# Convolution, attention and a sorted graph layer on one core: six images first, the gathers spread over four stages

## What is computed

```
def reference(x, ...):                      # x: (8, 56, 56, 64), float32
    # 1. 32 paths of 1x1 conv 64->4, 3x3 conv 4->4, 1x1 conv 4->64, each with batch norm and relu; summed
    x = relu(sum_over_paths(path(x)) + x)
    t = x.reshape(8, 3136, 64)
    # 2. attention, 8 heads, a 7 x 7 window around each pixel
    t = t + attention(layernorm(t))
    # 3. graph attention over 262144 random edges (src, dst < 16384), then a mixture of 4 experts
    z = layernorm(t).reshape(25088, 64)
    h = (z @ W_gat).reshape(M, HEADS, NUM_EXPERTS)
    a_src, a_dst = (h * att_src).sum(-1), (h * att_dst).sum(-1)
    e = leaky_relu(a_src[src] + a_dst[dst])             # every edge, and a loop on every node
    ee = exp(e - segment_max(e, dst)[dst])
    alpha = ee / segment_sum(ee, dst)[dst]
    agg = segment_sum(h[src] * alpha, dst) + b_gat
    w, k = top2(layernorm(agg).mean_over_heads)         # gates of two of four experts
    return t + sum_over_experts(gate[e] * (gelu(z @ W1[e] + b1[e]) @ W2[e] + b2[e]))
```

## Time and profile before

| | |
|---|---|
| median of 3 runs | 6876.4 us (6873.09 to 6878.02) |
| the profiled execution: time, span | 6868.53 us, 6867.0 us |
| busy PE, PEld | 2998.4 us, 2106.3 us |
| busy DVE, ACT, POOL | 3009.2 us, 1471.6 us, 3021.5 us |
| gathers L1483: busy, idle ahead of them | 2008.8 us, 990.0 us |

### The profile page before, as it was taken

One profiled execution on the slowest core, in us unless ns is written; L12 is line 12 of the kernel. 1 busy time (PEld: TensorE's weight loads), 2 busy tenths in 40 slices (PEclk: granted clock), 3 DMA queues, 4 the chain that ended last, 5 costly groups with the idle time before them and its releaser, 6 DMA issues. The chain is left out here.

```text
span 6867.0 us, 61389 instructions
## 1 busy us (share of the span) xinstructions
PE 2998.4 (44%) x16592; PEld 2106.3 (31%) x16592; DVE 3009.2 (44%) x4102; ACT 1471.6 (21%) x5678; POOL 3021.5 (44%) x3316
## 2 busy tenths in 40 slices
PE   2888888879999450000444231313121131314400
PEld 1444454468888340000333120202111120203200
DVE  5888888559999321011999020201111020202229
ACT  0333333468888220000000010100000010101100
POOL 1000000046767237776000767575757667572345
PEclk9788888779999555555555555555555555555555
DMA  6666666556666331000000011111111111111125
GB/s 138 89 92 94 96 95 96 83 90 102 103 101 102 87 91 8 9 7 7 3 4 3 13 46 16 33 24 33 28 32 25 15 46 15 34 24 47 49 70 198
DMA packets 584829, 385.88 MB, mean 56 GB/s; under 512 B 404739, under 2 KB 531507, under 8 KB 581715
## 3 DMA queue, kind: packets, MB, share of 16 engines
q1 hardware_dynamic: 385528, 221.54, 14.5%
q10 hardware_dynamic: 89403, 109.89, 9.2%
q0 software_dynamic: 109728, 52.69, 6.6%
HBM read 235.34 MB, written 147.70 MB: 56 GB/s over the span
## 5 line engine op out<-in xcount | busy, mean ns | idle before, releaser
L1483 POOL DMA_INDIRECT e_row<-scratch_table,e_edge x2048 | 2008.8, 981 | 990.0 <-issue 681.8
L1664 PE MATMUL f_psY<-f_w,f_hid 128*128 128x64 f32 x1568 | 363.1, 425 | 1649.5 <-ACT f_hid L1615 1052.8
L1547 DVE TENSOR_TENSOR f_y<-f_psY,f_b 128x1024 f32<-128x1024 f32 x49 | 59.8, 1220 | 2294.7 <-DMA scratch_vpad<-v 1432.9
L1664 PEld LDWEIGHTS f_psY<-f_w,f_hid 128*128 128x128 f32 x1568 | 342.6, 330 | 1741.9 <-ACT f_hid L1615 1117.1
L1522 DVE TENSOR_TENSOR i_hot<-f_psH,i_digit 128x1024 bf16<-128x1024 f32 x512 | 582.4, 1214 | 639.9 <-DMA scratch_b<-c_b3p 371.6
L1615 ACT ACTIVATE f_hid<-f_psH,f_b 128x512 f32<-128x512 f32 x196 | 131.4, 687 | 2920.5 <-PE f_psH L1659 1352.0
L1647 PE MATMUL f_psH<-i_hot 128*128 128x128 bf16 x2048 | 264.8, 310 | 958.2 <-DVE i_hot L1522 814.5
L947 POOL MEMSET a_wproj<- 128x128 f32 x1 | 0.2, 210 | 1368.4 <-POOLq L144 1368.4
L1060 ACT ACTIVATE prob<-psS,low 128x100 f32<-128x100 f32 x1568 | 514.1, 373 | 62.1 <-DVE low L1093 62.0
L1647 PEld LDWEIGHTS f_psH<-i_hot 128*128 128x128 bf16 x2048 | 197.2, 140 | 1025.7 <-DVE i_hot L1522 879.4
L455 PE MATMUL psH<-h,c_w 128*128 128x448 f32 x1008 | 508.7, 592 | 3.6 <-ACT h L567 1.8
(11 more groups left out here) (280 smaller groups left out, 5385.6 us busy)
## 6 DMA issues: line engine op xcount, KB each, us to landing
stack<-scratch_parts ACTq DMA_DIRECT2D x504, 112.0 KB
e_row<-scratch_table,e_edge POOLq DMA_INDIRECT x2048
scratch_y<-f_y ACTq DMA_DIRECT2D x49, 512.0 KB
g_y<-scratch_y SPq DMA_DIRECT2D x28, 896.0 KB, 4.9
scratch_state<-e_state SPq DMA_DIRECT2D x16, 1536.0 KB, 6.0
val<-scratch_vpad SPq DMA_DIRECT2D x672, 35.0 KB
scratch_parts<-h2p ACTq DMA_DIRECT2D x56, 336.0 KB, 3.8
keys<-scratch_kpad SPq DMA_DIRECT2D x112, 155.0 KB
```

The lines of the kernel that those rows point to most:

```text
L1483: pool.indirect_dma_start(out=row[s][:, f, :], out_offset=None, in_=table_dram, in_offset=bass.IndirectOffsetOnAxis(ap=edge[s][:, 0, f:f + ...
L1664: m = pe.matmul(psY[par][:, j, e * C:(e + 1) * C], hid[e][:, j * 128:(j + 1) * 128], w2[:, e, :], start=True, stop=True)
```

## The change

Images 0 to 5 go through convolution, attention and the table first (`FIRST_IMAGES = 6`). The rows that edges need are then all in the table. Images 6 and 7 go through the same three stages a second time, and POOL gathers meanwhile. The parts:

- A class `Gather` deals with the 2048 gathers in 32 units of 64. A unit has its list of sources (3 lists in a ring), one of 4 row buffers, and a store to DRAM. Four units run beside the second convolution, three beside the second attention, one beside the second table, eight beside the counting, and the last 16 after the scatter. The scans read the rows back from DRAM with SP's queue (`load_rows`).
- Weights of the convolution stay in the on-chip memory, so that the second call prepares nothing.
- In the second attention POOL does nothing but gather: SP loads all 10 rows of values, the residual's rows and stores the result.
- The sort has 11 slots a tile; its 429 steps after the prefix then need 39 tiles where they needed 48.
- The table stage is unrolled, with rings of 4 buffers in place of pairs, and the index steps stand between the steps of its chunks on DVE. In the second call squares and scaling are on DVE.
- Join and output are one stage, `finish_phase`: four blocks of columns, (128,196), (0,48), (48,96), (96,128); the first needs no gathered sums. Sums stay on the chip. Scaling, a sum by halves, and the residual are all on DVE, in chunks of 8.

```diff
-SORT_SLOTS = (5, 6, 7, 8, 9, 10, 11, 12, 13)
+SORT_SLOTS = (4, 5, 6, 7, 8, 9, 10, 11, 12, 13, 14)
...
+FIRST_IMAGES = 6
+UNIT = FC // 2
+UNITS = 2 * NFC
+CONV_UNITS, ATTENTION_UNITS, TABLE_UNITS, COUNT_UNITS = 4, 3, 1, 8
...
+    def gather(self, pool, count):
+
+        for unit in range(self.unit, self.unit + count):
+            if unit == 0:
+                for k in range(self.LISTS):
+                    self.load_list(pool, k)
+            s = unit % self.SLOTS
+            pool.wait_ge(self.list_in[unit % self.LISTS], 16 * (unit // self.LISTS + 1))
+            wait(pool, self.rows_out[s], 16 * (unit // self.SLOTS))
+            for f in range(UNIT):
+                pool.indirect_dma_start(out=self.row[s][:, f, :], out_offset=None, in_=self.table,
+                                        in_offset=bass.IndirectOffsetOnAxis(ap=self.list[unit % self.LISTS][:, f:f + 1].bitcast(I32), axis=0)
+                                        ).then_inc(self.rows_in[s], 16)
+            if unit > 0:
+                self.store(pool, unit - 1)
...
-    conv_phase(nc, io, t1, q, kpad, vpad, ordered)
-    attention_phase(nc, io, t1, q, kpad, vpad, t2)
-    index_phase(nc, io, ordered, digit, edge, first, ends)
-    table_phase(nc, io, t2, z, table, adst)
-    edge_phase(nc, io, z, table, adst, digit, edge, node, first, b, state, y)
-    join_phase(nc, io, state, node, first, ends, sums)
-    output_phase(nc, io, table, adst, sums, y, t2, out)
...
+            held = ConvWeights(nc, ctx)
+            conv_phase(nc, io, held, early, t1, q, kpad, vpad, sorted_dram=ordered)
+            attention_phase(nc, io, early, t1, q, kpad, vpad, t2, lasting=lasting)
...
+                table_phase(nc, io, early, t2, z, table, adst, index=index)
+            rows = Gather(nc, ctx, lasting, table[0:FIRST_IMAGES * H * W], edge, gathered)
+            conv_phase(nc, io, held, late, t1, q, kpad, vpad, rows=rows, units=CONV_UNITS)
+            attention_phase(nc, io, late, t1, q, kpad, vpad, t2, rows=rows, units=ATTENTION_UNITS)
+            table_phase(nc, io, late, t2, z, table, adst, rows=rows, units=TABLE_UNITS)
+            edge_phase(nc, io, rows, z, adst, digit, edge, node, first, b, state, y)
+        finish_phase(nc, io, state, node, first, ends, table, adst, y, t2, out)
```

More of the change, by code:

```diff
@@ L1280, in _ @@
+                for r in range(RING):
+                    sp.wait_ge(stored[r], stores(r + (COUNT - 1 - r) // RING * RING))
+                if index is not None:
+                    index.stored_all(sp)
             @block.vector
@@ L1500, in _ @@
                 pool.dma_start(b_dram.rearrange("(p x) h -> p x h", p=128)[:, 0, :], b_first[:]).then_inc(b_placed, 16)
[L1501 to L1503 removed]
+                rows.gather(pool, UNITS - rows.unit)
             @block.vector
```

1164 lines of the change are left out of this document (674 added, 490 removed).

## The result

The changed kernel takes 6906.91 us (6875.72 to 6911.66, 20 runs) beside 6869.66 us for the kernel before (6860.32 to 6880.72, 20 runs): ratio 1.0051, 95% interval 1.0044 to 1.0059. It is slower by half a per cent. The forecast was 6870, six microseconds less than before; the range held, the sign did not. On some (those numbered 11 and 12 on record), PE, ACT, DVE and SP are slowed while POOL gathers; on others (0, 1 and 2) they are not. I call the first the slowing kind and the others the free kind. Chip 2 was met at two times and chip 11 at two times, and each showed its kind again. Both kernels were first measured on the slowing kind.

What follows compares the result with a forecast made beforehand. Gathers were taken as almost serial, with PE at about a tenth of its rate beside them. The terms -244 - 206 - 140 + 637 + 528 + 145 - 571 - 155 = -6 gave 6870 us, range 6515 to 6980.

Steps and rivals of the forecast that it cites:

- first scores: Start of attention's scores after the early convolution of 42 tiles, 39 of them sorting: at 1172.9 us, a gain of 244.
- second convolution: Convolution of the last images beside 256 gathers: 3 + 347 + 11 + 276 = +637 us.
- second attention: Attention of the last images beside 192 gathers, SP bounding a strip at 8.4 us: 263 + 11 + 254 = +528 us.
- second table: Table stage of the last images beside 64 gathers and a store: 88, 11 and 46, together +145 us.
- edge stage, first gather to last tile: Counting, scatter, 1024 later gathers at 1364 us with stores, then 34 tiles at 15.53: 3313 us, a gain of 571.
- What bounds the kernel: Whole kernel: gathers hide little, PE at 10% of its rate in counting, 14% in tiles; their 2700 us almost serial.
- three terms: Work done beside the moved gathers: 71 us in second convolution, about 34 in second attention, 20 in second table.
- the sort: Early convolution: two more slots lengthen a sorting tile by 1.3 us, from 22.3 to 23.6 (23.1 to 24.5).
- The gather's price in the tiles: Edge stage behind the scatter: 1024 gathers at 1.304 us each and 16 stores at 1.8, together 1364 us.
- The table's chunk: Early table, with four buffers and shifted steps: 5.1 us a chunk (4.85 to 7.8), 117 for the stage, -102.
- Rival one: Slowdown belongs to the edge stage's loops; unrolled convolution and table run free: 6526, chance 0.08; attention too: 6289, chance 0.05.
- Rival two: Gathers in second convolution and attention queue behind other transfers, 1.6 us for 1.35: 7087, with half 6979; chance 0.12.

Runs made afterwards that it cites:

- e3: The kernel before with eleven sort slots a tile in place of nine, nothing else: 5938.3 us beside 5857.5, ratio 1.0132, on the free kind.
- e4: The changed kernel without the split, with nine slots and the kernel before's edge stage, on the free kind: 5612.5 us beside 5857.5 for the kernel before.
- e9: The same program as e4 on the slowing kind: 6624.7 us beside 6874.7 for the kernel before, ratio 0.9633.
- small stages: A program of its own without the layer's work, short unrolled pieces side by side, such as PE beside gathers: 1707.0 us on the free kind, 1871.4 on the slowing.
- e8: The changed kernel with its eight early units of gathers put behind the scatter, on the slowing kind: 6936.1 us beside 6874.7 for the kernel before.
- e16: The changed kernel with a 500-column memset behind every edge gather, small stages behind it, slowing kind: 8464.1 us in all, the layer done at 6357.5.

## Why the prediction was right and wrong

| step | forecast | measured | difference |
|---|---|---|---|
| first scores | 1172.9 | 1208.9 | +36 |
| first attention, first to last scores | 618 | 617 | -1 |
| from there to the second convolution's first gather | 165 | 174 | +9 |
| second convolution | 637 | 618 | -19 |
| second attention | 528 | 526 | -2 |
| second table | 145 | 115 | -30 |
| edge stage, first gather to last tile | 3313 | 3354 | +41 |
| from there to the end | 283 | 289 | +6 |

The forecast's column is counted for the profiled execution, whose sum is 6862.5; the measured one took 6900.8, 38 more (the rows' differences sum to 40, with their roundings).

**What bounds the kernel** was read rightly for this kind of chip: beside dense gathers PE does one instruction per 1.3 to 1.4 us, the gathers hide little, and moving 512 of them moves their cost. With and without gathers the late stages differ by 572 us for 667 us of gathers, and 95 us of progress stand where the prediction had 71 + 34 + 20 = 125 in its three terms.

**Two terms of the sum failed, and the sort is the first.** "It is nearer to the first; I take 1.3, so 23.6 (23.1 to 24.5)" was a choice between 0.8 and 4.2 us for two slots. They cost 2.4, and 24.7 lies outside the bound given. Over 39 sorting tiles this is +43, and +36 at the first scores. The lower end, 0.8, was the share of two slots in 22.3 - 18.9, and 18.9 is too short for an unsorted tile, as said above. A slot's own time on DVE sets a floor that the prediction didn't look at: DVE is busy 18.8 us a tile with nine slots and 710.03/850 x 24.7 = 20.6 with eleven, so two slots are 1.9 us of work by themselves, and the tile grew by more than that. DVE's idle 3.5 us took nothing in. In e3 DVE's `acc` waits 98 us for PE's `psE` in those 850 and PE's `psE` 95 us for `acc`, as in a chain through both engines in which a slot between two steps delays the next; that reading wasn't tried by itself.

**The gather's price in the tiles** is the second, and the larger. The prediction took 1.304 from the kernel before for all 1024. Measured, of the changed kernel:

```profile
L207 POOL DMA_INDIRECT r_row<-scratch_table,r_list x1024: 938/942/2304, 4652.6 to 6096.2; - x171
  issue: 444.7, 1024
```

and of the kernel before, in the same part:

```profile
L1483 POOL DMA_INDIRECT e_row<-scratch_table,e_edge x1536: 942/947/3360, 3978.9 to 6244.1; - x192
  issue: 505.0, 1530
```

0.43 us of gap a gather against 0.33, so 1024 of them and 16 stores took 1444 us, not 1364: +80. The kernel before's own edge stage, in e4 and e9, has 670 and 682 us of gaps on the two kinds of chip; the changed kernel's `Gather` has 623 and 811 to 858. One program's gathers pay on the slowing chip, the other's hardly. Why is open. Most of the first is in a loop on POOL and the second is unrolled, but the kernel before's first 512 gathers are unrolled too and have 0.35 us of gap each (176.8 of the 681.8 us of the earlier trace rows) where `Gather` has 0.41 beside the same counting (234.1 for 576). The counting and the tail were 16 and 23 us shorter than forecast and took some of it back.

**The total was near by luck.** With the edge stage's parts taken singly the errors are 131 us one way and 91 the other. Either of the two failed terms put right would by itself have turned the forecast's -6 into an increase.

**The table's chunk** was sized nearly rightly: 4.7 us a chunk in the middle of the stage, for 5.1 (4.85 to 7.8). But the stage's end, with the index steps' stores ahead of the last rows on SP's queue, wasn't costed: 22 us from PE's last instruction to the next stage's first DMA.

**The second attention's -2** hides errors both ways. A strip takes 9.5 us once the gathers are over, not 8.4: 590 score matmuls in the 200 us from 2900, 28 a strip, where the kernel before does 766 in 200. SP was named rightly as the bound, since its issues follow one another without a gap there (3000 to 3020), but 20 of them take 0.47 us each and not 0.385 to 0.42. Against these 31 us stand 192 gathers that took 247 us and not 263, and the rest at the start and the end of the stage.

**Rival one** was given little chance for the right reason. The unrolled convolution is slowed as loops are, at 1.25 us an instruction. The rule of the Trainium skill that a branch breaks the prefetch of instructions (page "Runtime: NRT & Kernel Launch", section "🔬 Instruction fetch mechanics") can't explain that, since neither this code nor the small stages have loops. The Trainium skill's page "SBUF — State Buffer", section "🔬 SBUF: two separate sides", has a rule that PE and ACT never wait on anyone. It is about the memory's ports; taken as a forecast that nothing slows PE, it holds on one kind of chip (0.03 us an instruction beside gathers) and not on the other (1.38). What the prediction couldn't see is that rival one's time was a matter of the chip: where nothing is slowed, the kernel before itself is 1000 us shorter and the change brings 10%.

**Rival two**, gathers that pay for the traffic of the stage beside them, was half right in kind: they paid, but in the tiles, not in the second convolution, where 256 took 339 us, 1.32 each.

**The balance** hides two large sums: 250 us gained by the table and end stage (e9), against a split that costs here, since the unsplit version is 280 us shorter than the changed kernel. The eleven slots are a part of the 280; in the unsplit kernel they cost 81 by themselves (e3). The place of the 512 gathers is worth 31 us to the split (e8 less the changed kernel: the late stages pay 572 and the edge stage saves 603). The rest, more starts and ends of stages, SP's longer queue and the dearer gathers, wasn't taken apart.

**Open:** what in the chip the gathers fill. The runs show that it takes indirect DMAs (plain ones 0.53 us apart don't do it, for 60 us on end in e16), that rows of 80 or 256 bytes make no difference, that PE and DVE then get about one instruction through per gather, whether alone or three engines at once (the small stage with all of them: 115, 118 and 117 in 150 us beside 119 gathers; ACT alone gets 186), and that it is gone at 1.67 us a gather. Not tried: fewer rows a gather, and why chips differ; five chips are few, and what is loaded on them could differ as well as the chips. Not tried either: whether the recording of the trace, one record an instruction, has a part in it. Every time in this document is of an execution whose span and clock were recorded.

## What to carry to other kernels

Count instructions per us of each engine in a stretch beside the thing that is to be hidden, and compare with the same code elsewhere: a tenth of the rate means that next to nothing is hidden, whatever the engines' idle time promises. Before moving work beside dense gathers, try a little space between them; on a chip that slows the others, 0.45 us more a gather bought 540 us; on one that doesn't, the same space cost 1100 (6347.9 against 5251.9). And measure on more than one chip where a profile shows idle time that waits for "issue": the same pair of kernels was 10% apart one way on one chip and 0.5% the other way on the next.

## What the runs showed of the hardware

- The chips of these runs differ: the same kernel takes 5852 to 5866 us on three of them and 6868 to 6875 on two. On the slowing kind, beside 128-row gathers 1.25 us apart, PE completes an instruction per 1.38 us, DVE per 1.39, ACT per 0.81, and SP issues a DMA per 0.94 us in place of 0.54.
- In the small stages the slowdown comes some 7 to 15 us after the first gather. PE does 0.7 instructions a us at 1.25 us a gather, 13.4 at 1.50 (at a granted clock of 0.56) and 25.4 at 1.58 (at 1.00); at 1.67 it does 35, as without gathers.
- With gathers spaced by a memset of 500 columns the counting takes 578 us on the slowing kind, in place of 1225 beside dense gathers, and 578 on the free kind.
- Two more sort steps of DVE between the steps of a convolution tile lengthen it by 2.4 us, though they are 1.9 us of work and DVE idles 16% of the time.
